# Two weight requests moved into the groups before their use, and every fourth copy of transposed probabilities moved from ScalarE to VectorE

## What is computed

```
q = (x @ Wq + bq).reshape(B, S, N_HEAD, HEAD_DIM).transpose(0, 2, 1, 3)
k = (x @ Wk + bk).reshape(...)...
v = (x @ Wv + bv).reshape(...)...
scores = jnp.einsum('bhqd,bhkd->bhqk', q / math.sqrt(HEAD_DIM), k)
scores = scores + attention_bias
scores = jnp.where(src_mask, -jnp.inf, scores.astype(jnp.float32))
probs = jax.nn.softmax(scores, axis=-1).astype(v.dtype)
ctx = jnp.einsum('bhqk,bhkd->bhqd', probs, v)
x = x + (ctx @ Wo + bo)
```

## Time and profile before

| | |
|---|---|
| median of 3 runs | 5019.55 us (5014.91 to 5022.92) |
| the profiled execution, its own time | 5020.92 us |
| its span, first to last instruction | 5018.9 us |
| mean granted TensorE clock | 0.93 of full speed |
| busy: TensorE, ScalarE, VectorE, GpSimd | 86%, 50%, 53%, 25% |
| DMA | 704 MB, mean 140 GB/s |

### The profile page before, as it was taken

How to read it: one execution, slowest core, us unless ns; L and a number is a source line. 1 busy time by engine, 2 the same in 40 slices (tenths; PEclk the granted TensorE clock), 3 DMA queues, 4 the chain that set the end, 5 groups by cost and what they waited for, 6 DMA issues and landing times.

```text
span 5018.9 us, 70808 instructions
## 1 busy us (share of the span) xinstructions
PE 4328.5 (86%) x25808; PEld 3077.7 (61%) x25808; DVE 2639.2 (53%) x5783; ACT 2488.5 (50%) x4700; POOL 1272.0 (25%) x637
## 2 busy tenths in 40 slices
PE   7995798888989898888989898888989898888887
PEld 3441566666757566666757576666767575666666
DVE  8981545455453646454553645454454636454553
ACT  0102454647374555646374555646374645546462
POOL 0000132231414132231414132322314142322313
PEclk9995899999999999999999999999999999999999
DMA  3323653536354544535354544535353645535351
GB/s 117 104 96 85 190 163 109 171 108 189 114 173 132 161 153 122 178 99 178 118 165 132 166 152 123 178 110 178 106 177 120 189 128 152 158 114 174 111 168 51
DMA packets 534759, 704.31 MB, mean 140 GB/s; under 512 B 45280, under 2 KB 254992, under 8 KB 534384
## 3 DMA queue, kind: packets, MB, share of 16 engines
q1 hardware_dynamic: 517520, 666.23, 44.6%
q10 hardware_dynamic: 16896, 33.56, 1.8%
HBM read 529.30 MB, written 35.72 MB: 113 GB/s over the span
## 4 chain that ended last, share of the span: by engine, by line
PE 55%; DVE 8%; SPq 7%; ACT 6%; DMA 6%; issue 5%; POOL 3%; ACTq 0%; POOLq 0%; DVEq 0%
PE bank L845 33%; PE bank L926 6%; SPq L536 6%; PE bank L890 5%; PE bank L914 4%; PE bank L949 3%; PE bank L915 3%; ACT prob L697 2%; ACT probT L718 2%; DMA w_raw<-in_L_cond_Wk 2%; DMA w_raw<-in_L_cond_Wo 1%; DVE parts L1196 1%; DMA stack<-parts 1%; PE bank L854 1%; DMA V<-in_L_cond_W 1%
## 5 line engine op out<-in xcount | busy, mean ns | idle before, releaser
L627 POOL TENSOR_TENSOR w<-w_raw,w 128x1024 fp32r<-128x1024 f32 x240 | 587.5, 2448 | 2224.8 <-ACT w L688 2093.2
L926 PE MATMUL bank<-ident,prob 128*128 128x128 f32 x4096 | 672.3, 290 | 181.8 <-ACT probT L718 173.4
L697 ACT ACTIVATE prob<-prob,low 128x512 f32<-128x512 f32 x1024 | 736.0, 719 | 176.8 <-DVE low L1117 176.8
L1196 DVE TENSOR_TENSOR parts<-gel,parts 128x512 fp32r<-128x512 f32 x256 | 261.8, 1023 | 893.4 <-ACT parts L813 893.4
L718 ACT ACTIVATE probT<-bank 128x512 f32<-128x512 f32 x1024 | 607.8, 594 | 242.8 <-PE bank L926 227.2
L926 PEld LDWEIGHTS bank<-ident,prob 128*128 128x128 f32 x4096 | 524.7, 150 | 317.4 <-ACT prob L697 190.2
L1117 DVE CUSTOM_DVE_ANT_0 prob<-bank,prob 128x512 f32<-128x512 f32 x1024 | 696.9, 681 | 0.0
L914 PE MATMUL bank<-stack 128*128 128x512 f32 x1024 | 505.7, 496 | 98.0 <-DMA stack<-parts 52.1
L1116 DVE COPY fence<-cur 128x1 f32<-128x1 f32 x1024 | 156.0, 152 | 695.5 <-PE bank L915 669.4
L845 PE MATMUL bank<-xT,stack 128*128 128x512 f32 x1920 | 492.2, 405 | 22.1 <-DVE xT L1088 11.0
L627 POOL TENSOR_TENSOR stack<-V,stack 128x1024 fp32r<-128x1024 f32 x144 | 353.0, 2453 | 595.8 <-ACT stack L688 592.2
(11 more groups left out here) (182 smaller groups left out, 5882.4 us busy)
## 6 DMA issues: line engine op xcount, KB each, us to landing
prob<-in_fside_Bx16xSxS SPq DMA_DIRECT2D x512, 512.0 KB, 4.9
stack<-parts SPq DMA_DIRECT2D x1024, 128.0 KB, 2.5
V<-in_L_cond_W SPq DMA_DIRECT2D x256, 256.0 KB, 3.6
w_raw<-in_L_cond_W SPq DMA_DIRECT2D x256, 256.0 KB, 3.0
field<-in_x SPq DMA_DIRECT2D x16, 1024.0 KB, 5.3
x<-total ACTq DMA_DIRECT2D x16, 1024.0 KB, 5.8
xin<-x SPq DMA_DIRECT2D x16, 1024.0 KB, 5.6
w_raw<-in_L_cond_Wv SPq DMA_DIRECT2D x64, 256.0 KB, 2.8
```

The lines of the kernel that those rows point to most:

```text
L627: pool.tensor_tensor(w[s][:, 1, :], w_raw[s], w[s][:, 0, :].bitcast(F32), ALU.subtract).then_inc(w_lo[s], 1)
L697: act.activation(prob[:, i, :], prob[:, i, :], ACT.Exp, bias=low[:, i:i + 1], scale=-1.0, accum_out=total[:, g % 2, i:i + 1]).then_inc(exp ...
L926: mm = t.transpose(turned[e % 2][:, k * P:(k + 1) * P], prob[:, i, k * P:(k + 1) * P], ident[:])
L1196: v.tensor_tensor(parts[:, 2 * (f % 2) + 1, :], gel[:, f % 2, :], parts[:, 2 * (f % 2), :].bitcast(F32), ALU.subtract).then_inc(g_lo, 1)
```

## The change

It does two things. The request for the raw Wq/Wk of group 3 is issued in group 0 ahead of the wait for the bias piece p = 5, not behind the whole group; likewise the request for the first half of Wo in group 1, not behind that group. And the copy of a turned entry with i % 4 = 3 is done by VectorE behind its score step, not by ScalarE; the waits and the signal are the same.

```
+DVE_TURN = 3
...
+                        if p == 5 and g == 0:
+                            load_qk(0, ITEMS[0] * b + W0_QK + 3, 3)
+                        if p == 5 and g == 1:
+                            load_rows(0, ITEMS[0] * b + W0_O, Wo, 0)
 
                         sp.wait_ge(probT_full, ENTRIES * b + entry(g, 2 * p + 1) + 1 + START)
                         load_bias(b, g + 1, p // 2, p % 2)
...
-                    group(b, 0)
-                    load_qk(0, ITEMS[0] * b + W0_QK + 3, 3)
-                    group(b, 1)
-                    load_rows(0, ITEMS[0] * b + W0_O, Wo, 0)
-                    group(b, 2)
+                    for g in range(G - 1):
+                        group(b, g)
...
-                        e = entry(g, i)
-                        act.wait_ge(probT_full, ENTRIES * b + e + 1 + START)
-
-                        act.wait_ge(pv_done, 64 * b + max(16 * g + i // 4 * 4 - 4, 0) + START)
-                        act.activation(probT[:, i % 8, :], turned[e % 2][:], ACT.Copy).then_inc(turned_copied[e % 2], 1)
+                        if i % 4 != DVE_TURN:
+                            e = entry(g, i)
+                            act.wait_ge(probT_full, ENTRIES * b + e + 1 + START)
+
+                            act.wait_ge(pv_done, 64 * b + max(16 * g + i // 4 * 4 - 4, 0) + START)
+                            act.activation(probT[:, i % 8, :], turned[e % 2][:], ACT.Copy).then_inc(turned_copied[e % 2], 1)
...
+                def copy_turned(b, g, i):
+                    e = entry(g, i)
+                    v.wait_ge(probT_full, ENTRIES * b + e + 1 + START)
+
+                    v.wait_ge(pv_done, 64 * b + max(16 * g + i // 4 * 4 - 4, 0) + START)
+                    v.tensor_copy(probT[:, i % 8, :], turned[e % 2][:]).then_inc(turned_copied[e % 2], 1)
...
                             score_step(b, g + 1, i + S_LEAD - 16)
+                        if i % 4 == DVE_TURN:
+                            copy_turned(b, g, i)
                         if i == 5 and not first:
```

## The result

| | before | after |
|---|---|---|
| median | 5019.97 us (4 runs, 5014.91 to 5022.92) | 4884.79 us (4 runs, 4877.47 to 4889.68) |
| ratio of after to before, 95% interval | | 0.9731 [0.9714, 0.9747] |
| span of the profiled execution | 5018.9 us | 4887.8 us |

A forecast was written before the change was run, and what follows sets the result against it. No engine is full; hand-overs bound the kernel: late weights at two boundaries, then stack pieces. 10.0 - 1.4 + 0.8 = 9.4 us per batch, times 16 = 150 us, gives 4871 us; own range 4850 to 4895, whole range 4830 to 4930.

The forecast's parts named there:

- Which limit goes and what is next: At both boundaries ScalarE's waits for Wk and Wo go; TensorE's last projection piece then releases the split, 0.3 us after ScalarE's last copy.
- The term of 10.0 us: Gain per batch from the earlier requests at the two boundaries: 5.1 us for Wk and 4.9 us for Wo.
- The landing: Moved requests land in time: Wk by 1703.3, before the split; Wo, with some 7 us for a 5.3 us transfer, less to spare.
- The duration of the new copy: Each of sixteen VectorE copies per batch, PSUM to SBUF, takes 0.69 us, with bounds of 427 and 748 ns.
- Group 3: ScalarE works without a break there; two copies leaving its stretch win 0.8 us per batch, bounds 0 and 1.4.
- The 6 us that the prediction priced for copies held by POOL: Entry 7's copy in group 3 held by the shared port: 0.4 us a batch, 6 us in all, left out of the sum.
- The cost of the copy ahead of the low part: At i = 3 VectorE's copy delays k's low part: 0.69 us in groups 1 and 2, -1.4 us per batch; nothing in group 0.
- Rival (a), the clock: Group 1 meets its stack pieces and TensorE falls to 1.2 GHz: 3 us per batch lost, 4919 us; chance 0.25.
- (b): The copy ahead of the low part is hidden: 11.4 us per batch gained, 4838 us; chance 0.10.
- (c): The DMA engines are the limit in the shorter groups, bias data delaying stack pieces: 70 us gained, 4951 us; chance 0.07.
- (d): Moved requests queue behind bias pieces and weights arrive no earlier; only the copies count: 22 us slower, 5043 us; chance 0.03.
- (e): The guard on slot 0 holds the moved requests until their old place: 5020 to 5043 us; chance 0.01.

The follow-up runs named there:

- requests_only: The changed kernel with all copies back on ScalarE, so only the requests are moved: 4862.64 us, ratio 0.9703 to the kernel before.
- requests_p7: The kernel of requests_only, with the two requests ahead of bias piece p = 7 instead of p = 5: 4916.33 us, ratio 0.9786 to the kernel before.
- after_again: The changed kernel, unaltered, measured once more on the third set's chip: 4885.53 us, ratio 0.974 to the kernel before.
- group3_again: The changed kernel with VectorE's copies in group 3 alone, second measurement, on the third set's chip: 4840.74 us, ratio 0.9655 to the kernel before.
- skip_again: The changed kernel with entry 3 of groups 0 to 2 back on ScalarE, second measurement, third set's chip: 4848.80 us, ratio 0.9669 to the kernel before.
- low_first: The changed kernel, but at i = 3 of groups 0 to 2 VectorE writes k's low part before its copy: 4857.16 us, ratio 0.9693 to the kernel before.

## Why the prediction was right, and where it was off

**Which limit goes and what is next: right.** ScalarE's waits for the two transfers went, and TensorE's projection was the next to release the split (0.95 us where the idle now also takes in the time of the copy that ScalarE no longer makes). The term of 10.0 us is 9.98 by the stages of requests_only, and 9.4 (8.9 to 9.8) by the medians of its set, so it may be up to a tenth too large. In group 1 two small shifts cancel, which the prediction did not have: from the split to the first stack piece takes 6.15 us in place of 5.76, and from there to entry 12 takes 13.07 in place of 13.49.

**The landing: right.** The raw Wk lands 0.85 us ahead of the split on average, where the prediction had 0.8 (1703.3 against 1704.1), and Wo 0.97 us, not with less to spare. In 2 of 16 batches the split still waited for Wo, 2.3 us in all. requests_p7 shows that the place has a margin of less than two bias pieces.

**The duration of the new copy: right.** 686 ns on average, 256 times (forecast 0.69), from a single row of the preparation.

**Group 3: right.** 19.61 to 18.81 us is the +0.8. The 6 us that the prediction priced for copies held by POOL and left out of its sum did not come: no copy took over 692 ns.

**The cost of the copy ahead of the low part: its kind right, its size too small.** The step that failed is the term "0.69 us in groups 1 and 2, where the stack pieces decide, -1.4 us per batch", with its bound of -1.5, together with "its pieces were not waited for; nothing" for group 0. Against requests_only the changed kernel is longer by 0.37 in group 0, 0.86 in group 1 and 1.50 in group 2, 2.73 us. On one chip, after_again against group3_again, it is 0.17, 0.58 and 2.00, 2.75 us in all and 2.8 by the medians. So group 1 costs about what the term said, and the excess is in group 2. With entry 3 on ScalarE (skip_again) group 2 is 1.17 us shorter; the other 0.83 belong to entries 7, 11 and 15, of which the prediction said that ScalarE's lead covers them. By the medians they cost 8 us of the 45, and the intervals overlap. From the split to the first piece it takes 0.64 and 0.57 more in groups 1 and 2 (6.79 and 6.77 us against 6.15 and 6.20): the copy. Of group 2's rest, 0.78 us is the stretch behind entry 12 (6.47 against 5.69), the low clock; on one chip it is 1.27 (6.66 against 5.39). Group 0's pieces had little slack: the wait there went from 0.08 to 0.30. The expected place of entry 12 in group 1, 20.5 us behind the split, is 20.1 (19.3 before).

**Rival (a), the clock: it came, but in another place and not by its own account.** It was expected in group 1, at 3 us a batch, since the shortened group 1 would meet its stack pieces. In requests_only that hardly happens: the wait in group 1 goes from 0.30 to 0.46 us. The copies bring it to 1.36, and group 1 still stays at full clock (its stretch behind entry 12 takes 5.60 to 5.62 us in all runs in which SyncE alone issues the pieces). Group 2, which I had taken as it was, has the low clock in 15 batches of 16, where it had it in 8. Had it been read in all 16 batches and not in one, a term for it could have stood in the sum; its size could not have been told from the kernel before.

**The other rivals.** (b): low_first shows that the copy is not hidden. (c): the pieces do load the DMA engines nearly fully, but requests_only with the same shortened groups keeps groups 2 and 3 within 0.15 us. (d) and (e) fell with the two waits.

**The balance.** 9.98 + 0.80 - 0.37 - 0.86 - 1.50 = 8.05 us a batch. That only divides the difference of two rows of the table, 8.04, and is no check of it. The medians give 8.4: by the ratios 9.3 for the requests, less 0.9 for all the copies together. The forecast had 9.4, from 10.0 and -0.6, and the 4885 us lie in its own range of 4850 to 4895. So the 14 us by which it was off have two sources that the runs can't divide sharply: the first term, up to 0.7 a batch too large by the ratios and exact by the stages, and the copies, 0.3 a batch too cheap by the ratios and 1.3 by the stages.

## What to carry to other kernels

When work is put ahead of an instruction that feeds a transfer, its own duration is not what it costs: here a copy of 0.69 us cost 0.5 us in group 1 and 1.2 in group 2 (after_again against skip_again), where more batches ran at the low clock of TensorE. Moving work from a loaded engine to an idle one pays only in the stretches that the loaded engine limits, and in a list written by hand its exact place counts: the copies of entry 3 cost 37 us on one chip, where the four of group 3 win about 13 to 18 by themselves. A state that an engine is in for part of the repetitions (a clock, here) is counted over all of them before its cost is put at nothing.

## What was not expected of the hardware

- Pieces of 128 KB within SBUF, 32 partitions each, fill the DMA engines (share 0.87 to 1.04) at 190 to 230 GB/s, while with bias pieces of 512 KB from memory they move 356 to 395 at shares of 0.97 to 1.04. A second issuer brought the rate from about 200 to 227 and the landing of the piece that was waited for from 2.4 to 6.2 us.
- POOL issued its pieces at 4.18 us for eight, 0.52 each. SyncE takes 0.64 for each when alone and 0.90 beside POOL (7.21 us for eight).
- TensorE's granted clock around waits of 2 to 5 us in all falls in some batches and not in others of the same execution, with the same program: 8 of 16 before, 15 of 16 after. How long a batch had waited does not tell which.
